# Dilation on unnormalised input, with the work of each chunk dealt anew to four engines and the DMA queue

## What is computed

```
def _gn(v, G=16, eps=1e-05):                 # groups of 2 channels
    m, s = mean(v), var(v)                   # over one image's group
    return (v - m) / sqrt(s + eps)

def dilation(u, kernel, r):                  # r = 5, 11 x 11 taps, padding -1e30
    for di, dj in 11 x 11:
        acc = max(acc, pad(u)[.., di:di+H, dj:dj+W] - kernel[c, di, dj])
    return acc

x = x + dilation(_gn(x), kernel, 5)
x = x + _L1_conv_ref(_gn(x), ...)            # projection, depthwise 3x3, norm, gelu, offsets, bilinear sampling
```

## Time and profile before

| | |
|---|---|
| median of 3 runs | 11006.0 us (11000.41 to 11007.82) |
| profiled execution | 11004.33 us, span 11002.5 us |
| mean granted TensorE clock | 0.935 |
| VectorE busy | 10525.9 us, 96% |
| ScalarE busy | 9775.8 us, 89% |
| GpSimd busy | 9105.1 us, 83% |
| TensorE matmul busy | 8451.1 us, 77% |
| dilation: first join to last join | 364.0 to 9188.9 us, 64 joins |

### The profile page before, as it was taken

How to read it: one execution, slowest core, us unless ns; L and a number is a source line. 1 busy time by engine, 2 the same in 40 slices (tenths; PEclk the granted TensorE clock), 3 DMA queues, 4 the chain that set the end, 5 groups by cost and what they waited for, 6 DMA issues and landing times. The chain is left out here.

```text
span 11002.5 us, 74894 instructions
## 1 busy us (share of the span) xinstructions
PE 8451.1 (77%) x17056; PEld 3258.3 (30%) x17056; DVE 10525.9 (96%) x5756; ACT 9775.8 (89%) x7129; POOL 9105.1 (83%) x2891
## 2 busy tenths in 40 slices
PE   1777777777777777777777777777777777887888
PEld 0222222222222222222222222222222222333333
DVE  8999999999999999999999999999999998998999
ACT  2999999999999999999999999999999997777666
POOL 2888888888888888888888888888888886666898
PEclk9999999999999999999999999999999998998999
DMA  7666666666666666666666666666666664443666
GB/s 289 130 128 128 127 123 127 126 125 123 131 130 130 128 128 124 126 127 129 128 130 128 129 128 128 128 127 129 130 128 127 126 127 128 160 162 148 250 252 251
DMA packets 387126, 1574.52 MB, mean 143 GB/s; under 512 B 20960, under 2 KB 127584, under 8 KB 324448
## 3 DMA queue, kind: packets, MB, share of 16 engines
q0 software_dynamic: 218256, 901.04, 45.5%
q1 hardware_dynamic: 168400, 668.43, 16.4%
HBM read 467.08 MB, written 201.33 MB: 61 GB/s over the span
## 5 line engine op out<-in xcount | busy, mean ns | idle before, releaser
L446 POOL TENSOR_TENSOR m_pool<-r_pool,u 128x2048 f32<-128x2048 f32 x1536 | 6776.4, 4538 | 920.3 <-ACT r_pool L540 867.2
L495 PE MATMUL chain<-dx,mats 128*128 128x512 f32 x6144 | 3119.5, 651 | 943.9 <-ACT chain L558 942.6
L643 DVE SCALAR_TENSOR_TENSOR acc_a<-m_pool,kt,acc_a 128x2048 f32<-128x2048 f32 x1472 | 3465.6, 2354 | 60.1 <-POOL m_pool L446 17.5
L495 PE MATMUL chain<-dx,neg_ident 128*128 128x512 f32 x4608 | 2419.1, 672 | 853.0 <-ACT chain L558 852.3
L643 DVE SCALAR_TENSOR_TENSOR acc_a<-u,kt,acc_a 128x2048 f32<-128x2048 f32 x960 | 2261.1, 2355 | 31.9
L540 ACT ACTIVATE r_pool<-dx,gap_l 128x2048 f32<-128x2048 f32 x1024 | 2051.7, 2004 | 72.5 <-POOL m_pool L446 33.2
L495 PEld LDWEIGHTS chain<-dx,mats 128*128 128x128 f32 x6144 | 1171.8, 202 | 2891.4 <-ACT chain L558 1741.1
L643 DVE SCALAR_TENSOR_TENSOR acc_a<-t,kt,acc_a 128x2048 f32<-128x2048 f32 x768 | 1808.2, 2354 | 22.8
L558 ACT ACTIVATE chain<-chain,gap_r 128x1024 f32<-128x1024 f32 x1536 | 1631.7, 1090 | 117.0 <-PE chain L495 116.8
L495 PE MATMUL chain<-u,mats 128*128 128x512 f32 x3072 | 1458.1, 606 | 217.9 <-ACT chain L558 217.9
L495 PEld LDWEIGHTS chain<-dx,neg_ident 128*128 128x128 f32 x4608 | 920.7, 211 | 2351.0 <-ACT chain L558 1460.8
(11 more groups left out here) (148 smaller groups left out, 6931.0 us busy)
## 6 DMA issues: line engine op xcount, KB each, us to landing
t<-u POOLq DMA_DIRECT2D x768, 1059.0 KB, 8.7
u<-x_dram SPq DMA_DIRECT2D x28, 3328.0 KB, 27.5
xw<-x_scratch SPq DMA_DIRECT2D x65, 1152.0 KB, 7.3
hw<-h_scratch SPq DMA_DIRECT2D x66, 1024.0 KB, 9.3
x<-xc POOLq DMA_DIRECT2D x65, 1024.0 KB, 8.9
xt<-x_dram SPq DMA_DIRECT2D x32, 2048.0 KB, 14.4
xc<-x_dram SPq DMA_DIRECT2D x64, 1024.0 KB, 4.8
x_scratch<-x SPq DMA_DIRECT2D x64, 1024.0 KB, 9.6
```

What stands on the lines that cost most here:

```text
L446: nc.gpsimd.tensor_tensor(m_pool[j % MP][:], r_pool[j % RP][:], u[s][:, k * CR + di:k * CR + di + CR, base:base + W], ALU.add).then_inc(m_ ...
L495: added = nc.tensor.matmul(chain[h][:, r:r + 2, :], weight, src[:, top:top + 2, dj:dj + W], start=False, stop=True, skip_group_check=True)
L643: nc.vector.scalar_tensor_tensor(out=acc_a[:], in0=src, scalar=k_base, in1=acc_a[:], op0=ALU.subtract, op1=ALU.max).then_inc(a_done, 1)
```

## The change

The dilation runs on x as read. A shift of the input doesn't alter which tap wins, and a scale can be put on the kernel: the tables `kt`, `nkt`, `gap_r` and `gap_l` are made for each group from the kernel times the standard deviation. So no window is normalised, and the rows of x that must be added are in `u`. The end of a chunk is two VectorE operations: the maximum of the accumulators into `acc_a`, then `x1 = acc_a * rstd + u` with an accumulator output for the sum. ScalarE only squares, in place. The second load of x, the adding DMA and `xc` go. The constant part of the shift is put into the tables of the later stages.

The work of a chunk is dealt anew. Chains: one left and five right, 58 steps in place of 54. Pairs: 16 by DMA in place of 12, 22 by GpSimd in place of 24, of which 3 (`CLAMPED`) have no ScalarE relu: GpSimd clamps `dx` itself (`tensor_scalar`, two operations) and then adds or subtracts. Single taps: 9 in place of 15. GpSimd's pairs now use one set of 4 buffers `m`, into which ScalarE writes the relu and GpSimd adds in place; `t` has 4 buffers.

GpSimd makes the differences of only the 16 new rows of a window (4 pieces, not 6); the 10 that it shares with the window before are copied by a DMA of SyncE. The rows outside the image are filled by a DMA from a constant tile. The loops are written out once for each group. All four orders are new.

```diff
-CHAINS = ((0, "left"), (1, "left"), (2, "left"), (3, "right"), (4, "right"), (5, "right"))
-NPOOL, NDMA = 24, 12
-ACT_ORDER = "rxr0x10r10r10r1bx10u10r1r01r0nx10r1x01r0n1r0r1xn01x0r10rn0x1r01rx0r10r1r01x0r1x01ru01x01r01r01r01"
-DVE_ORDER = "msssm10msmsmym10ymymssy1m0smsymmmsym01ysmmysmmym01mssysmmym10my"
-POOL_ORDER = "tttaditittditittdtititdittitttdititttidittt"
+CHAINS = ((0, "left"), (1, "right"), (2, "right"), (3, "right"), (4, "right"), (5, "right"))
+NPOOL, NDMA = 19, 16
+CLAMPED = (3, 11, 18)
+MP, TP = 4, 4
+ACT_ORDER = "xx0r10r10x10b1r0r10x10r10r10x1r0x10x1r01r0x10r1u0x10r10r10x10x1x0r10r1r01x01r01xx01r01r01r01x01"
+DVE_ORDER = "ms01mymsmysy0m1ymmsmyys0m1mmsymym0y1mssmmyym01ymysmymm0y1my"
+POOL_ORDER = "ciititttitdtititittitctittdiiitttiticitttit"
...
+                link(nc.vector.tensor_scalar(kt[:, g, :], ang[:], std[:, g:g + 1], None, ALU.mult))
...
+    NEXT_PIECES = ((10, 14), (14, 18), (18, 22), (22, UR))
...
+            def copy_shared(slot, w, g):
+                sp.wait_ge(dx_ready, pieces_done(g, w - 1))
+                sp.dma_start(dx[slot][:, 0:SHARED, :], dx[1 - slot][:, UR - SHARED:UR, :])
...
-                def add_x(c):
-                    pool.wait_ge(joined, c + 1)
-                    pool.wait_ge(xc_loaded, c * 16 + 16)
...
+                def clamp(c, s, k, i):
+                    pool.wait_ge(a_done, a_free(c, "m", j, NPAIR, MP))
+                    nc.gpsimd.tensor_scalar(m[j % MP][:], dx[s][:, top:top + CR, lo:lo + W],
+                                            gap_l[:, g, at_col:at_col + 1], FAR if right else -FAR,
+                                            first, second).then_inc(m_clamped, 1)
...
-                                    act.wait_ge(m_pool_ready, at(c, NPOOL, j + 1 - RP))
+                                        act.wait_ge(a_done, a_free(c, "m", relu_pairs[j], NPAIR, MP))
...
-                            nc.vector.tensor_tensor(x1[:], acc_a[:], acc_b[:], ALU.max).then_inc(joined, 1)
+                def join(c, s, k):
+                    nc.vector.tensor_tensor(acc_a[:], acc_a[:], acc_b[:], ALU.max).then_inc(merged, 1)
+                    dve.wait_ge(x1_squared, c + 1)
+                    dve.wait_ge(merged, at(c, 1, 1))
+                    passed(dve, dve_turns)
+                    nc.vector.scalar_tensor_tensor(out=x1[:], in0=acc_a[:], scalar=rstd[:, g:g + 1],
+                                                   in1=u[s][:, top:top + CR, R:R + W], op0=ALU.mult, op1=ALU.add,
+                                                   accum_out=sums1[:, 0, bass.ds(c + 1, 1)]).then_inc(joined, 1)
```

More of the change, by code:

```diff
@@ L83, in dilation_taps @@
             singles += [(di, 10)]
-    while len(pairs) > NPOOL + NDMA:
+    while len(pairs) > NPOOL + len(CLAMPED) + NDMA:
         di, base, outer = pairs.pop()
@@ L378, in window @@
[L378 to L380 removed]
+                        c = w * CPW + (g * GROUP_CHUNKS + k)
+                        sp.wait_ge(joined, c + 2)
                         passed(sp, sp_turns)
[L382 to L388, removed]
@@ new lines, in chunk @@
+                def chunk(c, s, k, w, ahead, loads):
+                    if k == 0 and CLAMPED:
+                        pool.wait_ge(dx_ready, pieces_done(g, w))
+                        pool.wait_ge(shared_copied, copies_done(g, w))
+                    for kind, j in numbered(POOL_ORDER):
+                        if kind == "t":
+                            pair(c, s, k, j)
+                        elif kind == "i":
+                            add_u(c, s, k, j)
+                        elif kind == "c":
+                            clamp(c, s, k, j)
+                        else:
+                            turn, turns = k * D_TURNS + j, CPW * D_TURNS
+                            for no in range(turn * len(ahead) // turns, (turn + 1) * len(ahead) // turns):
+                                if no == 0:
+                                    pool.wait_ge(win_loaded[1 - s], loads)
+                                difference(1 - s, ahead[no])
@@ new lines, in _ @@
+                pool.wait_ge(pads_set, 1)
+                pool.wait_ge(win_loaded[0], loads_done(0, 0))
+                for piece in FIRST_PIECES:
+                    difference(0, piece)
+                for g in range(GROUPS):
+                    with nc.Fori(0, WIN // 2 - 1, engines=POOL_ONLY) as i:
+                        for s in range(2):
+                            for k in range(CPW):
+                                chunk(i * CH_IT + (g * GROUP_CHUNKS + s * CPW + k), s, k, i * 2 + s, NEXT_PIECES,
+                                      loads_done(g, i + s))
+                    for w in (WIN - 2, WIN - 1):
+                        s = w % 2
+                        ahead = NEXT_PIECES if s == 0 else FIRST_PIECES if g + 1 < GROUPS else ()
+                        for k in range(CPW):
+                            chunk(g * GROUP_CHUNKS + w * CPW + k, s, k, w, ahead, loads_done(g, (w + 1) // 2))
@@ new lines, in _ @@
+                for g in range(GROUPS):
+                    with nc.Fori(0, WIN // 2, engines=DVE_ONLY) as i:
+                        for s in range(2):
+                            for k in range(CPW):
+                                c = i * CH_IT + (g * GROUP_CHUNKS + s * CPW + k)
+                                if k == 0:
+                                    dve.wait_ge(win_loaded[s], loads_done(g, i))
+                                    passed(dve, dve_turns)
+                                for kind, j in numbered(DVE_ORDER):
+                                    if kind in "01":
+                                        merge_chain(c, int(kind), j)
+                                    else:
+                                        merge(c, s, k, kind, j)
+                                join(c, s, k)
```

322 lines of the change are left out of this document (152 added, 170 removed).

## The result

The changed kernel takes 10809.5 us (10794.8 to 10814.3, 4 runs) against 11006.9 us: ratio 0.982, 95% interval 0.980 to 0.984. It is faster by 197 us. 10660 was forecast, with a range of 10570 to 10850: the direction and the range held, and of the 346 us of gain only 57% came.

What follows compares the result with a forecast made beforehand. VectorE was taken to set the dilation's 140.08 us chunk period; 5.2 us less for 64 chunks gives 335 us, and about 5 after the stage: 11004 - 335 - 5 = 10664, stated as 10660 us, range 10570 to 10850.

Steps and rivals of the forecast that it cites:

- VectorE after: VectorE's chunk: four merges fewer, a second join and its gaps added; floor from 138.86 to 132.65 us, 6.2 less.
- The rival of an accumulating join at half rate: VectorE's second join takes 2.36 us more a chunk, 151 us in all, giving 10810 us; chance 7%.
- ScalarE after: ScalarE's chunk: normalisation, one pass and a relu go, four chain steps come; busy from 132.8 to 129.4 us.
- halved margin: ScalarE's spare time in a chunk falls from 7.2 to 3.2 us, so waiting was raised from 1.2 to 2.2 us.
- GpSimd after: GpSimd's chunk: fewer pairs and differences, four more DMA issues, three clamps at 3.6 us; busy 124.0 us, from 121.2.
- GpSimd meets VectorE's floor at 6.5 us for a clamp: GpSimd's summed time stays under VectorE's 132.65 us unless a clamp exceeds 6.5 us; chance of that 10%.
- The prediction's signs of being wrong: VectorE waits naming late adds, GpSimd's pairs without GpSimd idle, or chain ends above 4 us; or a second join of 4.7.
- DMA: DMA engines in the dilation: sixteen adds take 96 of 133 us a chunk, some 80% busy, with landings hidden.
- the rival of late adds: Load and copy stretch an add from 8.7 to 19.7 us, VectorE waits 3 us a chunk more: 10850 us; chance 9%.
- TensorE: TensorE's chunk: 58 chain steps, busy 117 us at the mean clock of 0.93; it fits, more tightly.
- Sum: Chunk period: floor down 6.2 us, waits 2.2 where there were 1.2, period 134.85, 5.2 less; 335 us over 64 chunks.
- The forecast's own range of waits: VectorE's waiting of 0.5 to 4.5 us a chunk, giving 10550 to 10810 us.

Runs made afterwards that it cites:

- three edits: Changed kernel with minimum first in every clamp, each chunk's first difference later and the copy of shared differences later: 10517.0 us, ratio 0.956.
- The first run: Changed kernel with the right-hand clamp also written minimum first, maximum second: 10598.6 us, ratio 0.963.
- The second run: Changed kernel with each chunk's first difference two DMA issues and three pairs later in GpSimd's order: 10716.5 us, ratio 0.973.
- the run above: Kernel with all three edits, SyncE's store of a window's last chunk and the next load held back, first difference two pairs later: 10517.0 us, ratio 0.955.

## Why the prediction was right, and where it was off

**VectorE after.** Right, and a little pessimistic. 47 merges at 2.39 us, a second join of 2.35. The gaps ahead of the joins are 0.20 and 0.23 where I took 0.39 each, the accumulator's read takes 0.08 and nothing is held up by it, and the first merge follows 0.15 us later where I took 0.4. That is 0.8 us off the floor of 132.65; the floor was 130.8, by the shortest chunks with three edits. Some 0.7 more comes from the chunk that the sum started from: it took 138.86, and the shortest before the change took 138.2. The last 0.4 us are not accounted for. The rival of an accumulating join at half rate fell with this row.

**ScalarE after.** 129.4 forecast, 129.7 measured. Its halved margin was what I raised the waits for. That reason was wrong: no VectorE wait grew on that side (chain ends 65.8 us, 78.9 before).

**GpSimd after.** The sum was near, 124.0 against 125.5, and it hid a term that was mis-sized, the clamp: 3.6 us taken for each, 4.46 the mean, but really 2.0 to 4.4 for two and 7.1 to 9.0 for one. The nearest row could not tell that the order of two comparisons matters. The Trainium skill, "GPSIMD Engine Reference", section "Elementwise — side-by-side cycle accounting", led to an estimate of 3.1 us; the trace agrees with it in neither form, 1.96 us at best with the minimum first and 7.1 at best with the maximum first, and the measurement decides.

The step that failed is the comparison that followed: "GpSimd meets VectorE's floor at 6.5 us for a clamp". I read 124 against 132.65 as cover of 8.6 us for anything on GpSimd. But in the order a pair is merged soon after it is made, and VectorE waits for it in turn; a hold-up of 5 to 10 us at one place reaches VectorE, even when the engine has 11 us idle elsewhere in the chunk, which it spends waiting for relus that ScalarE makes later. The first run shows the size: 5.2 us less of GpSimd's time gave 3.3 us of period, with GpSimd not the busiest engine in either. The second run shows it without any change of the sum: GpSimd busy 125.5 us before and 125.6 after, and 1.5 us less of period, only by an operation that stands elsewhere. The prediction's signs of being wrong had the same gap. They name waits for `m` only "with GpSimd without idle time"; what came was waits for `m` with GpSimd idle for 11.6 us a chunk.

**The load.** The prediction looked at what the load does to the adds and not at who waits for the load. ScalarE's normalisation was that waiter before; the change removed it, put GpSimd in its place, and stood the first difference some 30 us into its order. The sum had no term for it. It cost 143.6 us of GpSimd's time and, by the second run, 93 us in all.

**DMA.** The engines' share came to 0.78 (80% forecast), and an add lands in 9.7 us in the median, 19.0 at most:

```profile
DMA to landing us min/median/max: 8.1/9.7/19.0
```

VectorE waited for none of them in the stage, three side by side or not. The layout of the orders held here, and the rival of late adds is refuted.

**TensorE.** Busy 112.8 us, not 117, as the granted clock rose from 0.93 to 0.96 in the stage while it did more. It was no bound.

**Sum.** The floor was 130.8 us (132.65 forecast), the waits 6.3 (2.2 forecast), the period 137.1 (134.85). The term that was mis-sized is the waits. Of its 6.3 us the slow clamp has 3.3 and the load 1.5, by their runs, and 1.7 are left with all three edits. Most of the rest is the loop's turn, 5 us in every fourth chunk. The forecast's own range of waits went to 4.5 us, and a floor set 1.9 us too high hid part of the miss. The outer range held because it reached to other rivals, not because one of them had the mechanism: that is luck, and so is it that the time is that of the rival with the accumulating join at half rate, 10810, which the row of the join refutes.

**The turn's stall** is explained in part. It hangs on the turn (half the turns, half the stalls) and not on the load or the copy. Why it is 5 us in the changed kernel and 0.8 to 1.1 before is open. That the sequencer can't run ahead past the self-waits of the second join would fit, but wasn't tried. Nor is it excluded that the engine waits for the first instructions of the loop's body: the run above only took SyncE's transfers out of the way. The traces bear on both. At each of 15 turns read (5 before the change, 4 after, 3 each with all three edits and with VectorE's loop turned half as often), one packet of the queue q14, which the profile calls instruction, stands 2.1 to 2.5 us ahead of the first merge. Three chunk starts without a turn have none, one of them a turn that was taken out. Before the change the packet comes 1.0 to 1.3 us after the join starts, while the join still runs; after it, 2.0 to 3.0 us after the second join has ended. So the stall would be a fetch that starts only when the second join is done. That is argued: the trace doesn't say whose instructions they are, and no run took the self-wait away.

## What to carry to other kernels

Idle time of an in-order engine is cover only where it stands: ask of each operation who waits for its successor and how soon, not whether the engine's sum stays under the bound. When work that waited for a transfer is removed, look for the operation that is first to need the transfer now. And before an operation without a row in the trace is dealt out, measure it alone in each form in which it will be used.

## What the hardware showed that was not expected

- GpSimd `tensor_scalar`, 128 x 2048 fp32, two comparisons: 1.96 to 4.4 us with the minimum first, 7.1 to 9.6 with the maximum first, whichever operand was the constant (3e38 or -3e38) and whichever the per-partition value.
- VectorE's accumulator output from a multiply-add with one PSUM and one SBUF operand cost nothing beyond its read of 0.08 us: 2.35 us, as without.
- One turn of VectorE's loop cost 4.9 to 5.3 us of issue time in the changed kernel and 0.8 to 1.1 before. With 6 turns for 14 the sum fell from 71 to 28.9 us.
